# A decoder layer on one core: each layer norm's four normalised tiles shared between GpSimd and ScalarE

## The chip, the cores and the metric

One core of one Trainium2 chip runs the whole kernel in one launch. The time is the device time of that core in microseconds, the median of three runs. In the rows PE is TensorE, PEld its weight load, DVE is VectorE, ACT is ScalarE, POOL is GpSimd and SPq is the queue of SyncE, which issues the DMAs.

## The reference

Four batch entries (b = 0 to 3) of 512 tokens and 128 channels pass through one decoder layer, all in f32. `_layernorm` has no learnt scale or bias.

```python
def _layernorm(x, axis=-1, eps=1e-05):
    m = jnp.mean(x, axis=axis, keepdims=True)
    v = jnp.var(x, axis=axis, keepdims=True)
    return (x - m) / jnp.sqrt(v + eps)

x = x + attn(_layernorm(x))            # causal, 16 heads of 8 channels
x = x + xattn(_layernorm(x), ctx)      # 77 masked context rows, 16 heads
x = x + ffn(_layernorm(x))             # gate, top 2 of 8 experts of 128x128, summed by weight
```

So there are twelve layer norms, named (b, k) here: k = 0 before the causal attention, 1 before the cross attention, 2 before the experts.

## The kernel before

The work is cut into some 530 steps. The string `ORDER` (line 66) holds one letter for each; `chains` (line 73) has a list of steps per letter, and `plan` (line 126) takes the next step of a letter's list each time the letter comes. A step is a triple (kind, b, k). The result, `SCHEDULE`, is one order for the whole program, and **every engine walks it in that order** and does its own part of each step: a loop over `SCHEDULE` stands in the block of SyncE, GpSimd, ScalarE, VectorE and TensorE. Engines meet at semaphores only. Digits in `ORDER` are steps "warm": products of ones on PE (line 929) whose results nobody reads.

PSUM has eight banks. `plan` gives each step on PE that needs one the bank (or pair) that is released earliest in the order, and PE waits in `bank_free` (line 885) until the engine that reads the bank's former contents has counted up `bank_taken`. So an activation or a reduction that reads a bank also decides when PE may begin a later step.

The steps that the text speaks of:

- `ln_stats`: DVE takes the statistics of four tiles of 128 tokens (lines 729 to 736) and signals `var_ready`; POOL makes `rstd` by a power (line 500) and `shift` = −mean · rstd (line 501), four columns each.
- `ln_norm`: POOL makes the four normalised tiles `normed` (line 508), each as state · rstd + shift, and signals `norm_ready`. There are two buffers of `normed`, so from the third norm on it waits for the turn before the last.
- `turn_x`: PE waits for `norm_ready` and transposes the four tiles into a bank (lines 939 to 942, recorded at line 909); ACT copies them to `normed_t` (line 604).
- `peak`: PE makes scores in one layout (lines 1009 and 1014) and DVE reduces them to maxima (line 764); `xpeak` is the same for the cross attention (line 779). Their halves are split by `split_peaks` and `split_xpeaks`.
- `scores`: PE makes the scores transposed, less their maximum, two banks at a time (line 1081); ACT takes the exponential of both banks into `probs` (line 664), 128x1024 each time; POOL masks it (line 558). `xscores` is the same for the cross attention (line 671). `values` and `xvalues` are the products with v (lines 1099 and 1121).
- `turn_mix` (ACT's copy at line 686), `add_attention` (PE at line 901, DVE adds to `state` at line 819), `gate`, `choose` (ACT's exponential at line 689, between two parts of DVE's), `expert` (PE at line 1151, DVE at line 870) and `sum_experts` (POOL at lines 569 and 572).

In the order, `ln_norm` stands 2 to 27 steps behind its `ln_stats` and 1 to 17 steps ahead of its `turn_x`. Before the change ACT has no part in it. Around norm (0, 1) the order is, for instance: ln_stats (0, 1), scores (1, (1, 1)), values, **ln_norm (0, 1)**, scores (1, (1, 2)), two peaks, context_values, scores (1, (1, 3)), values, scores (1, (1, 4)), ln_stats (3, 0), values, scores (1, (2, 0)), scores (1, (2, 1)), a peak, turn_x (0, 1). Norm (2, 1) stands right behind `choose` (0), and norm (3, 1) right behind `choose` (1).

Of the kernel before, what the change touches and what calls it, by code (L numbers as in the profile page):

```python
# [10 lines left out]
ALU = mybir.AluOpType  # L11
ACT = mybir.ActivationFunctionType
# [5 lines left out]
T = S // 128  # L18
# [39 lines left out]

XPROBS = 6
BANKS, CAUSAL_BANKS = 8, (6, 7)  # L60

SUMMED_BY_DVE = ((B - 1, 1), (B - 1, 3))

# [107 lines left out]
def uses(*kinds):  # L171

    return {x: n + 1 for n, x in enumerate(x for x in SCHEDULE if x[0] in kinds)}


STATS = uses("ln_stats")
NORM = uses("ln_norm")
NORMS = list(NORM)


def decoder_layer(nc, x, ctx_t, mask, wq, bq, wk, bk, wq_t, bq_t, wk_t, bk_t, wv, bv, wp, bp, xwq, xwk,
                  xwv, xwo,
                  gate_w, gate_b, expert_w, expert_b, out):
    with ExitStack() as stack:
        def sb(name, shape, dt=F32):
            return stack.enter_context(nc.sbuf_tensor(name, shape, dt))

        def sem(name):
            return stack.enter_context(nc.semaphore(name))
# [36 lines left out]
        state = sb("state", [128, B, T, D])  # L226
# [4 lines left out]
        rstd = sb("rstd", [128, 3 * B, T])  # L231
        lowered = sb("lowered", [128, 3 * B, T])
        shift = sb("shift", [128, 3 * B, T])
        normed = sb("normed", [128, 2, T, D])
# [62 lines left out]
        last_row_ready = sem("last_row_ready")  # L297
        causal_full, causal_ready = sem("causal_full"), sem("causal_ready")
        var_ready, norm_ready = sem("var_ready"), sem("norm_ready")
        bank_full = [sem(f"bank_full{i}") for i in range(BANKS)]  # L300
        bank_taken = [sem(f"bank_taken{i}") for i in range(BANKS)]
        q_ready = sem("q_ready")
# [38 lines left out]
        def bank_of(step, s=0):  # L341
            return banks[:, PLACE[step] + s]
# [4 lines left out]
        def full_of(step):  # L347
            return bank_full[PLACE[step]]

        def taken_of(step):  # L350
            return bank_taken[PLACE[step]]

        def wait_full(eng, step):

            eng.wait_ge(full_of(step), FULL[step])
# [12 lines left out]
        def context_heads_of(b):  # L368
            return xv_s[0:S2, b, VW:].rearrange("p (h c) -> p h c", c=2 * VW)
# [94 lines left out]
        def _(pool):  # L464
            gp = nc.gpsimd
            chain = [0]

            def link(ins):
                chain[0] += 1
                ins.then_inc(pool_chain, 1)  # L470
                pool.wait_ge(pool_chain, chain[0])
# [22 lines left out]
            for step in SCHEDULE:  # L494
                kind, b, k = step
                if kind == "ln_stats":

                    n = 3 * b + k
                    pool.wait_ge(var_ready, STATS[step])
                    link(gp.tensor_tensor(rstd[:, n], var[:, n], minus_half[:], ALU.pow))  # L500
                    link(gp.tensor_tensor(shift[:, n], lowered[:, n], rstd[:, n], ALU.mult))
                elif kind == "ln_norm":
                    n = 3 * b + k
                    i = NORM[step]
                    if i > 2:
                        wait_full(pool, ("turn_x", *NORMS[i - 3][1:]))
                    for t in range(T):
                        last = gp.tensor_scalar(normed[:, i % 2, t], state[:, b, t], rstd[:, n, t:t + 1], shift[:, n, t:t + 1],  # L508
                                                ALU.mult, ALU.add)
                    last.then_inc(norm_ready, 1)  # L510
# [3 lines left out]
                elif kind in PROJECTED:  # L514
                    n = PROJECTED[kind]
# [5 lines left out]
                elif kind in SPLIT:  # L521
                    n = SPLIT[kind]
                    pool.wait_ge(middle_ready[n], b + (2 if n == "x" else 1))
                    gp.tensor_tensor(parts[n][:, 2], rest_of(n, b), parts[n][:, 1], ALU.subtract).then_inc(low_ready[n], 1)
                    if kind == "split_k" and b == 0:
# [5 lines left out]
                        for e in range(E):  # L531
                            last = gp.memset(rank[:, :, e:e + 1], float(E - e))
# [27 lines left out]
                elif kind == "sum_experts" and (b, k) not in SUMMED_BY_DVE:  # L560

                    t = k
# [13 lines left out]
        def _(act):  # L576
            ac = nc.scalar
# [16 lines left out]
            for step in SCHEDULE:  # L594
                kind, b, k = step
                if kind == "context_values":
                    wait_full(act, step)
                    if b == 0:
                        wait_cleared(act, "xv_s")
                    ac.copy(context_heads_of(b)[:, :, 0:DH], bank_of(step)[0:S2, 0:D].rearrange("p (h d) -> p h d", h=H)  # L600
                            ).then_inc(taken_of(step), 1)
                elif kind == "turn_x":
                    wait_full(act, step)
                    ac.copy(normed_t[k][:], bank_of(step)).then_inc(taken_of(step), 1)  # L604
# [4 lines left out]
                elif kind == "project_qt":  # L609
                    act.wait_ge(bias_ready, 1)  # L610
                    wait_full(act, step)
                    for i in range(GROUPS):
                        ac.activation(q_t[:, i], bank_of(step), ACT.Identity, bias=q_bias[:, i:i + 1],
                                      scale=own[:, i:i + 1]).then_inc(q_ready if i < 3 else taken_of(step), 1)
                elif kind in PROJECTED:
                    n = PROJECTED[kind]
# [13 lines left out]
                    else:  # L630
# [5 lines left out]
                        bias = (bq_s if n == "q" else bk_s)[:, 0:1]  # L636
                        ac.activation(parts[n][:, 0], bank_of(step), ACT.Identity, bias=bias).then_inc(high_ready[n], 1)
                        ac.activation(full[n][:], bank_of(step), ACT.Identity, bias=bias).then_inc(taken_of(step), 1)
                elif kind in SPLIT:
                    n = SPLIT[kind]  # L640
# [16 lines left out]
                elif kind == "scores":  # L657
                    grp, u = k
                    wait_full(act, step)
                    n = 4 * b + grp  # L660
# [5 lines left out]
                elif kind == "xscores":  # L666
                    wait_full(act, step)
                    n = H * b + 2 * k
# [213 lines left out]
        def _(pe):  # L882
# [22 lines left out]
            def turn(src, step):  # L905

                bank_free(step)
                for t in range(T):
                    last = te.transpose(bank_of(step)[:, 128 * t:128 * t + 128], src(t), ident[:])  # L909
                last.then_inc(full_of(step), 1)  # L910
# [8 lines left out]
            for c in range(2):  # L919
                last = te.matmul(banks[:, CAUSAL_BANKS[1], 128 * c:128 * c + 128],  # L920
                                 spread_slot[:, c].rearrange("p s r -> p (s r)"), causal[:, 0], start=True, stop=True)
            last.then_inc(causal_full, 1)

            for step in SCHEDULE:
                kind, b, k = step
# [13 lines left out]
                elif kind == "turn_x":  # L939
                    i = NORM[("ln_norm", b, k)]  # L940
                    pe.wait_ge(norm_ready, i)
                    turn(lambda t: normed[:, i % 2, t], step)
                elif kind == "project_kt":
                    wait_taken(pe, ("turn_x", b, 0))
# [21 lines left out]
                elif kind == "tile_peak":  # L966

                    grp, i, j = k
# [20 lines left out]
                    for t, col in TILE_PEAKS[i]:  # L989
                        last = te.matmul(bank[:, col:col + 128 * (t + 1)], lane(q_t, j)[:, grp, 128 * t:128 * t + 128],  # L990
                                         lane(k_t, j)[:, 0:128 * (t + 1)],
                                         start=False, stop=(t, col) == TILE_PEAKS[i][-1], skip_group_check=True)
                    last.then_inc(full_of(step), 1)
                elif kind == "peak":

                    f, u = k
                    t, heads = PEAKS[u]
                    n, width = len(heads), 128 * (t + 1)
# [13 lines left out]
                    for i, p in enumerate(heads):  # L1012
                        for s in range(2):
                            last = te.matmul(bank_of(step, s)[:, width * i:width * i + width],  # L1014
                                             in_slot(q_stack, s, MAX_ROW)[:, b % 2, 4 * f + p, 128 * t:128 * t + 128],
                                             in_slot(k_stack, s, MAX_ROW)[:, b % 2, 4 * f + p, 0:width],
                                             start=False, stop=(i == n - 1), skip_group_check=True)
                            if i == n - 1:
                                last.then_inc(full_of(step), 1)
                elif kind == "xpeak":  # L1020
# [11 lines left out]
                    if b in XDIRECT:  # L1032
# [6 lines left out]
                        for t in range(lo // 4, (hi + 3) // 4):  # L1039
                            first, end = max(lo, 4 * t), min(hi, 4 * t + 4)  # L1040
                            for s in range(2):
                                last = te.matmul(bank_of(step, s)[:, S2 * (first - lo):S2 * (end - lo)],  # L1042
                                                 in_slot(full["x"], s, SLOT)[:, 128 * t:128 * t + 128],
                                                 in_slot(own_keys, s, SLOT)[:, 4 * f + first - 4 * t:4 * f + end - 4 * t],
                                                 start=False, stop=(end == hi), skip_group_check=True)
                                if end == hi:
                                    last.then_inc(full_of(step), 1)
                    else:
                        for i in range(lo, hi):
                            t, p = divmod(i, 4)  # L1050
                            for s in range(2):
                                last = te.matmul(bank_of(step, s)[:, S2 * (i - lo):S2 * (i - lo) + S2],
                                                 in_slot(xq_stack, s, MAX_ROW)[:, b % 2, 4 * f + p, 128 * t:128 * t + 128],
                                                 in_slot(xk_stack, s, MAX_ROW)[:, 4 * f + p, S2 * b:S2 * b + S2],
                                                 start=True, stop=True)
                                if i == hi - 1:
                                    last.then_inc(full_of(step), 1)
                elif kind in ("turn_peaks", "turn_xpeaks"):
# [5 lines left out]
                    for t in range(T):  # L1064
                        last = te.transpose(bank_of(step)[0:16, 64 * t:64 * t + 64].bitcast(BF16),
                                            src[:, k, t].rearrange("p s i a -> p (s i a)"), ident_b[:])
                    last.then_inc(full_of(step), 1)
                elif kind == "scores":
# [9 lines left out]
                    for even, odd in zip(SCORES[2 * u], SCORES[2 * u + 1]):  # L1078
                        for s, (col, j, kt) in enumerate((even, odd)):
                            p, n = (4 * grp + j) // 2, S - 128 * kt  # L1080
                            last = te.matmul(bank_of(step, s)[:, col:col + n],  # L1081
                                             in_slot(k_stack, s)[:, b % 2, p, 128 * kt:128 * kt + 128],
                                             in_slot(q_stack, s)[:, b % 2, p, 128 * kt:S], start=True, stop=True)
                            if even == SCORES[2 * u][-1]:
                                last.then_inc(full_of(step), 1)
                elif kind == "values":
# [9 lines left out]
                    for kt in tiles:  # L1096
                        for j in range(4):
                            slot, col = PROB_PLACE[(kt, j)]
                            last = te.matmul(bank_of(step)[32 * j:32 * j + 2 * VW, 128 * kt:S], padded(v_s[:, b % 2, kt], 4 * grp + j),  # L1099
                                             probs[:, grp % 2, slot, col:col + S - 128 * kt], start=(kt == 0 and grp % 2 == 0),  # L1100
                                             stop=(kt == 2 and grp % 2 == 1), skip_group_check=True)
# [11 lines left out]
                elif kind == "xvalues":  # L1113
# [6 lines left out]
                    for j in range(4):  # L1120
                        last = te.matmul(bank_of(step)[32 * j:32 * j + 2 * VW, :], padded(xv_s[0:S2, b], 4 * k + j),  # L1121
                                         xprobs[0:S2, (H * b + 4 * k + j) % XPROBS], start=(k % 2 == 0), stop=(k % 2 == 1),
                                         skip_group_check=True)
                    last.then_inc(full_of(step), 1)
                elif kind in ("mix", "xmix"):
                    i = int(kind == "xmix")
# [13 lines left out]
                elif kind == "expert_bias":  # L1140
# [4 lines left out]
                    for t in range(T):  # L1145
                        last = te.matmul(bank_of(step)[:, D * t:D * t + D], comb_t[:], expert_b_s[:, t], start=True, stop=True)
                    last.then_inc(full_of(step), 1)
                elif kind == "expert":
                    bank_free(step)
                    t, half = divmod(k, 2)  # L1150
# [47 lines left out]
```

## Time and profile before

| what | value |
|---|---|
| median of three runs | 279.82 us (278.49 to 280.61) |
| the profiled execution | 279.67 us |
| its span in the trace | 277.6 us |
| mean granted clock of TensorE | 0.97 |
| instructions | 6416 |

The span is from the first to the last instruction of the program that the trace holds; the profiled execution's time is 2.07 us longer. Times in rows count from the start of the span.

### The profile page before, as it was taken

How to read it: one execution, taken by the hardware profiler on the slowest of the kernel's cores; microseconds unless marked ns; L12 is line 12 of the kernel's file. 1: busy time of each engine (PE TensorE's matmuls, PEld its weight loads, DVE VectorE, ACT ScalarE, POOL GpSimd, SP SyncE). 2: the span in 40 equal slices, each digit the busy share in tenths (PEclk: the TensorE clock that was granted, in tenths of full speed). 3: DMA queues.
4: the chain of work that ended last, by engine and by line, in shares of the span. 5: the costliest groups of instructions: out<-in, count | busy, mean ns of one | idle time of the engine just before them, and what ended most of it. 6: DMA issues, size and time to landing. Idle time of an engine off the chain costs nothing.

```text
span 277.6 us, 6416 instructions
## 1 busy us (share of the span) xinstructions
PE 253.6 (91%) x2438; PEld 121.3 (44%) x2438; DVE 227.1 (82%) x502; ACT 169.4 (61%) x225; POOL 162.2 (58%) x265
## 2 busy tenths in 40 slices
PE   7799778999998999999999999999999979997990
PEld 3379433434453354454345443345534643343540
DVE  7349999898999999999799998568986797355695
ACT  5183089698887768989979758983566334610000
POOL 5739676845549643766413582375985674059644
PEclk9899999999999999999999999999999995999797
DMA  3743326200440400611300001300003011000101
GB/s 86 208 114 104 104 68 171 61 15 6 109 122 2 113 6 5 183 49 33 85 5 6 2 0 40 81 4 2 5 0 94 21 42 40 2 0 0 38 0 38
DMA packets 19948, 14.32 MB, mean 52 GB/s; under 512 B 2720, under 2 KB 19920, under 8 KB 19920
## 3 DMA queue, kind: packets, MB, share of 16 engines
q1 hardware_dynamic: 19920, 13.94, 18.4%
q8 instruction: 19, 0.31, 0.5%
q14 instruction: 9, 0.07, 0.1%
HBM read 2.58 MB, written 1.05 MB: 13 GB/s over the span
## 4 chain that ended last, share of the span: by engine, by line
PE 46%; DVE 34%; ACT 5%; POOL 5%; issue 4%; SPq 2%; DMA 2%; DVEq 0%; POOLq 0%
DVE peaks L764 10%; PE banks L1099 8%; PE banks L1121 5%; PE banks L897 5%; PE banks L1151 5%; DVE peaks L772 5%; PE banks L1081 4%; PE banks L901 4%; PE banks L909 4%; ACT probs L664 3%; PE banks L1111 2%; DVE xpeaks L779 2%; PE banks L1014 2%; DVE stats L730 2%; DVE yw L870 2%
## 5 line engine op out<-in xcount | busy, mean ns | idle before, releaser
L664 ACT ACTIVATE probs<-banks 128x1024 f32<-128x1024 f32 x80 | 79.8, 1025 | 15.5 <-PE banks L1081 14.4
L764 DVE TENSOR_REDUCE peaks<-banks 128x2 f32<-128x768 f32 (+3 forms) x77 | 82.6, 1119 | 5.0 <-PE banks L1014 4.4
L558 POOL TENSOR_SCALAR_AFFINE_SELECT probs<-probs 128x512 f32<-128x512 f32 (+1 forms) x80 | 43.6, 549 | 52.3 <-ACT probs L664 51.6
L569 POOL TENSOR_TENSOR yw<-yw 128x512 f32<-128x512 f32 (+2 forms) x42 | 34.9, 830 | 22.3 <-DVE yw L870 19.4
L1099 PE MATMUL banks<-probs,v_s 128*18 128x256 f32 (+3 forms) x512 | 42.9, 436 | 0.0
L671 ACT ACTIVATE xprobs<-banks 77x1024 f32<-77x1024 f32 x32 | 31.9, 1017 | 11.7 <-PE banks L1111 11.6
L1151 PE MATMUL banks<-expert_w_s,normed_t 128*128 128x512 f32 x64 | 33.0, 620 | 0.0
L1081 PE MATMUL banks<-q_stack,k_stack 64*128 64x512 bf16 (+3 forms) x256 | 30.1, 300 | 1.8 <-DMA q_stack<-peaks_t 0.6
L779 DVE TENSOR_REDUCE xpeaks<-banks 128x10 f32<-128x770 f32 (+1 forms) x24 | 23.5, 1007 | 5.7 <-PE banks L1042 3.1
L1014 PE MATMUL banks<-k_stack,q_stack 62*128 62x128 bf16 (+3 forms) x224 | 27.3, 297 | 0.0
L870 DVE TENSOR_TENSOR yw<-banks,g_comb 128x512 f32<-128x512 f32 x32 | 20.8, 684 | 5.7 <-PE banks L1151 5.3
L1009 PE MATMUL banks<-causal_slot,pick_slot 64*128 64x64 bf16 (+2 forms) x308 | 19.5, 205 | 2.7 <-DVE peaks L764 1.8
L1009 PEld LDWEIGHTS banks<-causal_slot,pick_slot 64*128 64x128 bf16 x308 | 10.9, 94 | 24.1 <-DVE peaks L764 9.9
L508 POOL TENSOR_SCALAR normed<-state,rstd,shift 128x128 f32<-128x128 f32 x48 | 21.0, 451 | 0.6
L1099 PEld LDWEIGHTS banks<-probs,v_s 128*18 128x18 f32 x512 | 10.9, 97 | 17.6 <-issue 15.1
L1121 PE MATMUL banks<-xprobs,xv_s 77*18 77x512 f32 x128 | 18.3, 645 | 0.1
L1081 PEld LDWEIGHTS banks<-q_stack,k_stack 64*128 64x128 bf16 x256 | 9.4, 94 | 20.5 <-DVE peaks L764 6.7
L500 POOL TENSOR_TENSOR rstd<-var,minus_half 128x4 f32<-128x4 f32 x12 | 12.2, 1015 | 6.7 <-DVE lowered L736 6.7
L604 ACT COPY normed_t<-banks 128x512 f32<-128x512 f32 x12 | 7.0, 586 | 13.9 <-PE banks L909 13.8
L1151 PEld LDWEIGHTS banks<-expert_w_s,normed_t 128*128 128x128 f32 x64 | 10.8, 194 | 9.3 <-issue 8.7
L929 PE MATMUL banks<-ones_b 128*128 128x512 bf16 x46 | 14.1, 438 | 0.5 <-DVE peaks L764 0.5
L772 DVE TENSOR_REDUCE peaks<-banks 128x1 f32<-128x128 f32 (+3 forms) x32 | 12.8, 473 | 0.0
(179 smaller groups left out, 422.3 us busy)
## 6 DMA issues: line engine op xcount, KB each, us to landing
q_stack<-parts_q SPq DMA_DIRECT2D x24, 128.0 KB, 2.4
k_stack<-parts_k SPq DMA_DIRECT2D x24, 128.0 KB, 2.4
xq_stack<-parts_x SPq DMA_DIRECT2D x24, 128.0 KB, 2.4
state<-in_x SPq DMA_DIRECT2D x4, 256.0 KB, 4.9
out<-state SPq DMA_DIRECT2D x4, 256.0 KB, 2.3
expert_w_s<-in_expert_w SPq DMA_DIRECT2D x1, 512.0 KB, 4.3
xk_stack<-parts_x SPq DMA_DIRECT2D x6, 77.0 KB
q_stack<-peaks_t SPq DMA_DIRECT2D x16, 8.0 KB
```

Source lines behind the costliest of these rows:

```text
L558: gp.affine_select(out=v, in_=v, compare_op=ALU.is_ge, fill=0.0, base=0, pattern=pattern, channel_multiplier=-1).then_inc(causal_done, 1)
L569: link(gp.tensor_tensor(y[:, 0:n], y[:, 0:n], y[:, n:2 * n], ALU.add))
L664: ac.activation(probs[:, grp % 2, 2 * u:2 * u + 2, :], both_banks(step), ACT.Exp, scale=SCALE).then_inc(taken_of(step), 1)
L671: ac.activation(xprobs[0:S2, n % XPROBS:n % XPROBS + 2, :], both_banks(step)[0:S2], ACT.Exp, scale=SCALE).then_inc(taken_of(step), 1)
L764: ve.tensor_reduce(peaks[:, f, t, heads[0]:heads[0] + n].rearrange("p a s -> p s a"), both_banks(step)[:, :, 0:n * width].rearrange("p s ( ...
L779: ve.tensor_reduce(xpeaks[:, f].rearrange("p s t a -> p s (t a)")[:, :, lo:hi], both_banks(step)[:, :, 0:(hi - lo) * S2].rearrange("p s (h ...
L1009: te.matmul(half, in_slot(pick_slot, s, SLOT)[:, 128 * c:128 * c + 128], in_slot(causal_slot, s, SLOT)[:, c].unsqueeze(1).broadcast_to([SL ...
L1014: last = te.matmul(bank_of(step, s)[:, width * i:width * i + width], in_slot(q_stack, s, MAX_ROW)[:, b % 2, 4 * f + p, 128 * t:128 * t + 128],
L1081: last = te.matmul(bank_of(step, s)[:, col:col + n], in_slot(k_stack, s)[:, b % 2, p, 128 * kt:128 * kt + 128], in_slot(q_stack, s)[:, b % ...
L1099: last = te.matmul(bank_of(step)[32 * j:32 * j + 2 * VW, 128 * kt:S], padded(v_s[:, b % 2, kt], 4 * grp + j), probs[:, grp % 2, slot, col: ...
L1121: last = te.matmul(bank_of(step)[32 * j:32 * j + 2 * VW, :], padded(xv_s[0:S2, b], 4 * k + j), xprobs[0:S2, (H * b + 4 * k + j) % XPROBS], ...
L1151: te.matmul(bank_of(step), normed_t[2][:, 128 * t:128 * t + 128], expert_w_s[:, 4 * half:4 * half + 4].rearrange("d e f -> d (e f)"), star ...
```

## The change

Four things change. POOL's `shift` instruction now signals a semaphore `shift_ready`, in place of a link in POOL's own chain. In `ln_norm` POOL waits for it and makes tiles 0 and 1 only. ACT gets a part of `ln_norm`, at that step's place in the order: it waits for the buffer (from the third norm on) and for `shift_ready`, makes tiles 2 and 3 as `Identity` activations with the scale `rstd` and the bias `shift`, and signals `norm_ready_by_act`. PE's `turn_x` waits for both signals. `ORDER` stays as it is.

```diff
+NORM_BY_POOL, NORM_BY_ACT = (0, 1), (2, 3)
...
+        shift_ready, norm_ready_by_act = sem("shift_ready"), sem("norm_ready_by_act")
...
                     link(gp.tensor_tensor(rstd[:, n], var[:, n], minus_half[:], ALU.pow))
-                    link(gp.tensor_tensor(shift[:, n], lowered[:, n], rstd[:, n], ALU.mult))
+                    gp.tensor_tensor(shift[:, n], lowered[:, n], rstd[:, n], ALU.mult).then_inc(shift_ready, 1)
                 elif kind == "ln_norm":
                     n = 3 * b + k
                     i = NORM[step]
                     if i > 2:
                         wait_full(pool, ("turn_x", *NORMS[i - 3][1:]))
-                    for t in range(T):
+                    pool.wait_ge(shift_ready, STATS[("ln_stats", b, k)])
+                    for t in NORM_BY_POOL:
                         last = gp.tensor_scalar(normed[:, i % 2, t], state[:, b, t], rstd[:, n, t:t + 1], shift[:, n, t:t + 1],
                                                 ALU.mult, ALU.add)
                     last.then_inc(norm_ready, 1)
...
+                elif kind == "ln_norm":
+                    n = 3 * b + k
+                    i = NORM[step]
+                    if i > 2:
+                        wait_full(act, ("turn_x", *NORMS[i - 3][1:]))
+                    act.wait_ge(shift_ready, STATS[("ln_stats", b, k)])
+                    for t in NORM_BY_ACT:
+                        last = ac.activation(normed[:, i % 2, t], state[:, b, t], ACT.Identity, bias=shift[:, n, t:t + 1],
+                                             scale=rstd[:, n, t:t + 1])
+                    last.then_inc(norm_ready_by_act, 1)
                 elif kind == "turn_x":
...
                     pe.wait_ge(norm_ready, i)
+                    pe.wait_ge(norm_ready_by_act, i)
                     turn(lambda t: normed[:, i % 2, t], step)
```

## Rows read from the trace of the kernel before

**Rows 1.** Busy time in stretches: us, then PE, PEld, DVE, ACT, POOL, PEclk, DMA

```profile
0.00:277.60 277.60, 253.65 (x2438) 121.30 (x2438) 227.12 (x502) 169.41 (x225) 162.17 (x265) 0.97 0.19 52
...
81.00:88.00 7.00, 6.54 (x92) 2.76 (x84) 6.83 (x24) 6.34 (x8) 5.09 (x10) 1.00 0.01 2
```

**Rows 2.** The chain that ended last, share of the span by engine

```profile
PE 46%; DVE 34%; ACT 5%; POOL 5%; issue 4%; SPq 2%; DMA 2%; DVEq 0%; POOLq 0%
```

**Rows 3.** Timeline around norms (0, 0) and (3, 2): start, us, engine, what, [idle before]

```profile
9.78 0.44 PE L909 MATMUL banks<-ident,normed 128*128 128x128 f32 x2 [1.28 <-POOL normed L508]
...
253.52 1.74 POOL L508 TENSOR_SCALAR normed<-state,rstd,shift 128x128 f32<-128x128 f32 x4
...
255.31 0.66 PE L909 MATMUL banks<-ident,normed 128*128 128x128 f32 x4 [1.74 <-POOL normed L508]
```

**Rows 4.** ACT's groups by form: xcount | busy us, mean ns | idle before

```profile
L604 ACT COPY normed_t<-banks 128x512 f32<-128x512 f32 x12 | 7.0, 586 | 13.9 <-PE banks L909 13.8
...
L613 ACT ACTIVATE yw<-banks,q_bias,own 128x512 f32<-128x512 f32 x4 | 2.8, 776 | 1.0 <-PE banks L897 1.0
...
L600 ACT COPY xv_s<-banks 77x128 f32<-77x128 f32 x4 | 1.1, 271 | 0.5 <-PE banks L937 0.4
```

**Rows 5.** Timeline of ACT behind norm (3, 0) and behind norm (2, 2)

```profile
97.82 1.02 ACT L664 ACTIVATE probs<-banks 128x1024 f32<-128x1024 f32 x1 [0.94 <-PE banks L1081]
...
226.29 1.02 ACT L671 ACTIVATE xprobs<-banks 77x1024 f32<-77x1024 f32 x1 [4.36 <-PE banks L1111]
```

**Rows 6.** Timeline of ACT and POOL around norm (2, 0)

```profile
51.05 1.02 ACT L664 ACTIVATE probs<-banks 128x1024 f32<-128x1024 f32 x1 [0.69 <-PE banks L1081]
...
50.92 0.20 POOL L501 TENSOR_TENSOR shift<-lowered,rstd 128x4 f32<-128x4 f32 x1
```

**Rows 7.** Timeline of ACT, POOL, PE and DVE around norm (0, 1)

```profile
81.96 1.02 ACT L664 ACTIVATE probs<-banks 128x1024 f32<-128x1024 f32 x1
...
83.85 0.20 POOL L501 TENSOR_TENSOR shift<-lowered,rstd 128x4 f32<-128x4 f32 x1
...
83.04 0.39 PE L1081 MATMUL banks<-q_stack,k_stack 64*128 64x128 bf16 x4
...
87.38 1.21 DVE L764 TENSOR_REDUCE peaks<-banks 128x4 f32<-128x1024 f32 x1
```

**Rows 8.** Timeline of ACT, POOL and DVE around norm (1, 1)

```profile
121.17 1.03 ACT L664 ACTIVATE probs<-banks 128x1024 f32<-128x1024 f32 x1
...
122.73 0.20 POOL L501 TENSOR_TENSOR shift<-lowered,rstd 128x4 f32<-128x4 f32 x1
...
123.55 1.21 DVE L764 TENSOR_REDUCE peaks<-banks 128x4 f32<-128x1024 f32 x1
```

**Rows 9.** Timeline of ACT and PE around norms (0, 2) and (2, 1)

```profile
160.15 1.02 ACT L671 ACTIVATE xprobs<-banks 77x1024 f32<-77x1024 f32 x1 [0.23 <-PE banks L1111]
...
166.67 0.23 ACT L689 ACTIVATE g_exp<-g_shifted 128x32 f32<-128x32 f32 x1 [2.06 <-DVE g_shifted L834]
...
166.31 0.66 PE L909 MATMUL banks<-ident,normed 128*128 128x128 f32 x4
```

**Rows 10.** Timeline of ACT, POOL and DVE around norm (1, 2)

```profile
194.45 1.02 ACT L671 ACTIVATE xprobs<-banks 77x1024 f32<-77x1024 f32 x1 [1.41 <-PE banks L1111]
195.91 0.58 ACT L686 COPY mixed_t<-banks 128x512 f32<-128x512 f32 x1 [0.44 <-PE banks L909]
...
195.69 0.20 POOL L501 TENSOR_TENSOR shift<-lowered,rstd 128x4 f32<-128x4 f32 x1
...
198.33 0.69 DVE L819 TENSOR_TENSOR state<-banks,state 128x512 f32<-128x512 f32 x1
```

**Rows 11.** Busy time in stretches, columns as in rows 1

```profile
226.60:229.90 3.30, 2.17 (x18) 1.59 (x18) 1.90 (x4) 2.70 (x4) 2.90 (x5) 1.00 0.00 0
230.00:236.70 6.70, 6.70 (x27) 1.28 (x26) 5.58 (x24) 2.27 (x3) 2.69 (x4) 0.50 0.13 42
```

**Rows 12.** What PE's turns of the normed tiles waited for: us, times

```profile
  POOL normed L508: 12.9, 11
```

## The prediction

> **What bounds the kernel now.** I read the busy time of the whole span first [rows 1]: the reader is to see that no engine is idle for long, PE above all (253.65 of 277.60 us), then DVE (227.12), while ACT and POOL have 108 and 115 us to spare. Then the chain that ended last [rows 2]: almost half of it is PE, a third DVE, ACT and POOL 5% each. So average load says that ACT could take 24 small operations for nothing. But the stretch from 81 to 88 us, in which a layer norm falls, shows ACT busy for 6.34 of 7.00 us beside DVE at 6.83 [rows 1]: what counts there is the order in each queue, so I read the timelines around each of the 12 norms last. I write (b, k) for the norm k of batch entry b.
>
> The profiled execution took 279.67 us for a span of 277.6; the median of the three runs is 279.82, so I add my sum to 279.67 and take the two as the same.
>
> **What an operation costs.** POOL makes its four tiles in 1.74 us [rows 3] at the last norm, about 0.44 each; two are left, so POOL is done 0.88 us sooner, 12 times. The activation of a 128x128 tile with a scale and a bias from memory isn't in the trace. Nearest rows [rows 4]: a plain copy of 128 columns takes 0.271 us, one of 512 columns 0.586, the activation of 512 columns with both vectors 0.776. The vectors thus cost 0.19, and I take 0.46 for one. Four of the long ones keep ACT 2.8 us busy, 0.1 less each than their durations, so I take 0.82 for the pair; the bounds are 0.5 (two plain copies, overlapping) and 1.5 (two of the long ones). 24 of these add some 10 us to ACT's 169.41.
>
> The Trainium skill, Perfetto Trace Analysis, section Optimizing GPSIMD Operations, says to prefer other engines, since GpSimd is generally slower. The trace doesn't bear this out for this operation: 0.44 us on POOL against 0.46 estimated on ACT. By the rule the move would be a gain for its own sake; by the rows it is one only where both halves run at once.
>
> **Where the halves do run at once.** Norm (0, 0): PE stood idle for 1.28 us until POOL's last tile, and its turn starts at 9.78 [rows 3]; ACT had nothing to do. Both halves are there 0.88 us sooner: −0.9 us, and the chain goes on through PE and DVE, so it stays. Norm (3, 2), at the end: PE idle for 1.74 us for it [rows 3], ACT idle: −0.9 us again, up to the last store. Norm (1, 0) finds ACT idle, and what follows waits for DVE: 0. Norm (3, 0): ACT reaches it at 96.87 (97.82 less the idle 0.94), the shift is long ready, and 0.82 fits before the activation that had to wait for PE anyhow [rows 5]: 0. Norm (2, 2): ACT had 4.36 us idle before 226.29 [rows 5], and PE would be freed by 0.3, but what is next, the split maxima of the cross attention, waits for DVE: 0.
>
> **Where ACT comes too early.** The other seven have the step ahead of the activations that PE and DVE live on, and ACT is in order: behind its new wait stand the exponentials that empty the PSUM banks, behind those PE (in order too) for a bank, and DVE for PE's next maxima.
>
> Norm (2, 0): ACT is free at 50.36 (51.05 less the idle 0.69), the shift ends at 51.12, so the next scores start at about 52.0 instead of 51.05 [rows 6]. Their bank is wanted by PE a step later; DVE has maxima in hand. I take +0.4 (0 to 1).
>
> Norm (0, 1): ACT goes straight from one exponential to the next at 81.96, but the shift ends at 84.05 [rows 7]. The tiles are done at 84.95 and scores(1, (1, 2)) runs to 86.0 instead of 82.98, 3.0 us later. PE's scores step at 83.04 takes that very bank, so PE stands until 86.1. Then ACT has three more exponentials of 1.02 us one behind the other (they end at 87.6, 88.9, 89.8); PE's next peak step needs the bank of the second, starts at 88.95, and DVE's reduction of it, at 87.38, becomes 89.5: +2.1, because DVE had 1 us of statistics in hand. From there PE's next steps wait for DVE's reductions, so 2.1 is what goes on.
>
> Norm (1, 1): ACT goes on without idle time at 121.17, the shift ends at 122.93 [rows 8], tiles done at 123.85; scores(2, (1, 4)) starts 2.7 us later and frees its bank at 124.9. PE's next peak step takes that bank, and DVE's reduction of it, at 123.55, moves to 125.5: +2.0. The two exponentials behind are late by 2.3 to 2.7. I take +2.1.
>
> Norms (0, 2) and (2, 1): ACT reaches the first at 159.92, 0.82 of tiles where 0.23 was idle, so the activations behind it are 0.6 late, PE with them (it has no idle time to give back here). The second stands behind the gate's exponential, which ends at 166.90 because DVE gave its input late; PE's turn of those tiles was at 166.31 [rows 9]. It becomes 167.2 + 0.9 + 0.1 = 168.2: +1.9 for both, on PE, which is back to back from there to 190 us.
>
> Norms (1, 2) and (3, 1): ACT is free at 193.04 (194.45 less the idle 1.41), the shift ends at 195.89, tiles 196.8, and then the exponential that had run from 194.45 ends at 197.8. The copy of the mixed heads at 195.91 starts there: +1.9, PE's projection waits for it (+2.0), and the residual's addition on DVE, which begins at 198.33 [rows 10] on a bank that was ready some 0.6 us before, moves by +1.4. Stats, gate and top-2 follow, +1.6 where DVE releases the first expert bank. Norm (3, 1) is behind the gate's exponential as (2, 1) was, 1 us more on ACT, but PE is held by DVE later. I take +1.6.
>
> Sum: −0.9 − 0.9 + 0.4 + 2.1 + 2.1 + 1.9 + 1.6 = +6.3 us.
>
> **The clock.** PE gets new idle times of 3.0, 2.2 and 2.0 us in full speed stretches. In the kernel before, PE was busy for 2.17 of the 3.30 us up to 229.9, and the stretch after it, 230 to 236.7 us, was granted 0.50, that is 1.2 GHz in place of 2.4 [rows 11]. The Trainium skill, TensorE: Matmul & The Clock Gate, section Part 1: The HAM clock gate, has the gate follow how busy PE has recently been; the trace agrees, by this row. A stall of 3 us is a bigger hole than that one. What a fall costs: PE works 6.7 us at half speed, so between 0 (where DVE or ACT sets the pace) and 3.3 us each. I take 1.4 us in all, one fall that is half felt. Total +7.7: 287.4 us.
>
> POOL's 10 us are worth nothing but this: its masks and expert sums come 0.9 us sooner behind a norm, and the values steps that wait for masks then wait for ACT.
>
> **Rivals.** (a) *Absorbed waits.* The stalls are real but PE and DVE take back half of them between norms. For it: ACT idles about 108 us in all. Against it: PE and DVE, which would have to catch up, are at 6.54 and 6.83 of 7.00 around a norm [rows 1]. Half of 8.1 less 1.8 is +2.3 to +3.5: 282 to 283.2 us. (b) *Falls of the clock at each of the three long stalls,* fully felt, 1.7 to 3 us each: 6.3 + 6: 292 us. (c) *Faster: parallel halves decide.* PE was idle for 12.9 us before 11 turns, waiting for POOL's last tile [rows 12]; if ACT's halves are always there first, four turns on the chain and the two ends give 0.88 each, and the delayed exponentials cost less than that: 279.7 − 4 × 0.88 = 276.2 us. It decides only if ACT reaches its step no earlier than about 1 us before the shift; the rows show 2.1, 1.8 and 2.85 us at three norms, and at two it is behind the gate's exponential instead. (d) *Nothing:* the two ends (−1.8) pay for what isn't absorbed: 279 to 281 us. (e) The pair costs 1.5 us: that is in the range.
>
> **Chances.** The forecast (284.5 to 290.5) 0.58; (a) 0.20; (b) 0.09; (c) 0.05; (d) 0.08. The range, 282.4 to 292.3, takes in (a)'s upper half and most of (b), and the bounds of the pair. A per cent is 2.8 us, about what a measurement of this kernel can tell from no change: above 282.6 us lie the forecast, (b) and most of (a), 0.85; below 277.0 lies (c), 0.05; 0.10 between.
>
> **What would show it.** Per step: POOL's groups with 24 tiles of 0.44 us; ACT's new group of 24 at 0.4 to 0.5 us, with idle time before it of about 0.8 + 2.2 + 1.7 + 2.9 us at the four and more at idle places, released by POOL's shift; PE before scores (L1081's successor) waiting for ACT's probs at about 83 to 86 us; the start 0.9 us sooner up to 50 us; PE's clock at 0.5 in a stretch soon after a stall. DVE busy time unchanged, its idle time up by some 7 us. The prediction is wrong if DVE's reduction after norm (0, 1) is under 1 us late against the start's gain, if ACT's wait at (0, 1) or (1, 1) is under 1 us, or if the ends gain nothing.

## The result, and the profile after

The changed kernel took 285.2 us in the median of four runs (284.64 to 286.82), the kernel before 279.15 (276.67 to 280.61) beside it: a ratio of 1.0253, with a 95% interval of 1.0199 to 1.0308 (the quotient of the two medians is 1.0217). It is slower, by 2.5% where 2.8% was forecast (7.7 on 279.67), and the time lies in the range. Here and below, executions more than 1.5% above the fastest of their kernel stay in the medians and are left out of the ratios. The profiled execution took 285.58 us.

Busy time over the span, the lines of the page that say where load went (columns: busy us, share, instructions; then tenths of full clock in 40 slices), with the chain that ended last and three groups:

```profile
span 283.6 us, 6422 instructions
PE 252.2 (89%) x2433; PEld 120.6 (43%) x2438; DVE 227.3 (80%) x502; ACT 179.1 (63%) x249; POOL 152.1 (54%) x241
PEclk9999999999986999997999999999999999899998
PE 44%; DVE 30%; ACT 10%; POOL 7%; issue 6%; SPq 1%; DMA 1%; ACTq 0%; POOLq 0%; DVEq 0%
L779 DVE TENSOR_REDUCE peaks<-banks 128x2 f32<-128x768 f32 (+3 forms) x77 | 82.6, 1120 | 14.1 <-PE banks L1030 13.5
L1097 PE MATMUL banks<-q_stack,k_stack 64*128 64x512 bf16 (+3 forms) x256 | 31.3, 310 | 4.5 <-ACT probs L679 2.9
L614 ACT ACTIVATE normed<-state,shift,rstd 128x128 f32<-128x128 f32 x24 | 10.5, 486 | 25.9 <-POOL shift L505 25.8
```

Against [rows 1] and [rows 2]: 10 us of work went from POOL (162.17 to 152.11) to ACT (169.41 to 179.15), as meant; PE and DVE do what they did. But ACT's share of the chain doubled, and DVE's peak reductions, the group with the most busy time, now stand idle for 14.1 us, 13.5 of them until PE's scores; in the kernel before it was 5.0. The last row is ACT's new group: 0.486 us for one activation, and 25.8 us of idle time that POOL's shift ended, at eight norms. 17.9 of these fall on (0, 0), (1, 0), (2, 2) and (3, 2), where ACT had nothing else to do; 0.85, 2.30, 1.75 and 2.96 us fall on (2, 0), (0, 1), (1, 1) and (1, 2). PEclk shows two dips in the middle, at slices 12 to 13 and 19, that the kernel before had not.

The timeline of the changed kernel around norm (0, 1), ACT, POOL, PE and DVE (start, us, engine, what, [idle before <-releaser]), answers to [rows 7]:

```profile
78.73 1.01 ACT L679 ACTIVATE probs<-banks 128x1024 f32<-128x1024 f32 x1
82.03 0.88 ACT L614 ACTIVATE normed<-state,shift,rstd 128x128 f32<-128x128 f32 x2 [2.30 <-POOL shift L505]
82.82 1.00 ACT L679 ACTIVATE probs<-banks 128x1024 f32<-128x1024 f32 x1
...
81.74 0.20 POOL L505 TENSOR_TENSOR shift<-lowered,rstd 128x4 f32<-128x4 f32 x1
...
83.87 0.61 PE L1097 MATMUL banks<-q_stack,k_stack 64*128 64x128 bf16 x4 [2.94 <-ACT probs L679]
84.41 1.91 PE L1115 MATMUL banks<-probs,v_s 128*18 128x384 f32 x16
...
89.53 2.95 DVE L779 TENSOR_REDUCE peaks<-banks 128x4 f32<-128x1024 f32 x3 [4.91 <-PE banks L1030]
```

The reader is to see the whole mechanism in the brackets: ACT idle for 2.30 us until POOL's shift, PE idle for 2.94 until ACT's exponential frees a bank, DVE idle for 4.91 until PE has made its scores. PE's first matmuls behind the stall take 0.61 us where the same ones took 0.39 [rows 7]: the clock has fallen.

Busy time in stretches around the two stalls (columns as in rows 1):

```profile
80.00:82.90 2.90, 0.94 (x20) 0.50 (x12) 2.87 (x9) 0.86 (x3) 2.17 (x5) 1.00 0.02 6
83.00:89.70 6.70, 5.83 (x46) 1.89 (x47) 1.72 (x11) 4.26 (x6) 3.08 (x5) 0.50 0.00 0
...
122.00:127.20 5.20, 3.17 (x40) 1.88 (x34) 3.48 (x13) 3.45 (x6) 3.47 (x7) 1.00 0.01 3
127.30:130.60 3.30, 3.30 (x28) 0.89 (x24) 1.69 (x4) 2.51 (x3) 0.79 (x2) 0.50 0.00 0
```

Behind each of the two stalls, in which PE was busy for a third and for three fifths of the time, a stretch was granted 0.50 (1.2 GHz in place of 2.4), 6.7 and 3.3 us long. In the first DVE fell to 1.72 of 6.70 us, while PE, once it had the bank at 83.87, was busy to the end: PE is the bound there.

### The profile page after: what moved, and what is told of

It reads as the page before. It is cut to its first block, busy times and chain, and to the rows that moved or that the text cites. A ratio compares the mean times of both kernels' runs of the same rounds, so it can differ in the third digit from the quotient of the medians.

```text
span 283.6 us, 6422 instructions
## 1 busy us (share of the span) xinstructions
PE 252.2 (89%) x2433; PEld 120.6 (43%) x2438; DVE 227.3 (80%) x502; ACT 179.1 (63%) x249; POOL 152.1 (54%) x241
## 4 chain that ended last, share of the span: by engine, by line
PE 44%; DVE 30%; ACT 10%; POOL 7%; issue 6%; SPq 1%; DMA 1%; ACTq 0%; POOLq 0%; DVEq 0%
PE banks L1115 9%; DVE peaks L779 8%; PE banks L912 5%; PE banks L1137 5%; PE banks L1097 5%; DVE peaks L787 4%; ACT probs L679 4%; PE banks L916 4%; PE banks L924 3%; PE banks L1167 3%; PE banks L1030 3%; POOL yw L574 3%; PE banks L1025 2%; POOL rstd L504 2%; DVE xpeaks L794 2%
## 5 line engine op out<-in xcount | busy, mean ns | idle before, releaser
L779 DVE TENSOR_REDUCE peaks<-banks 128x2 f32<-128x768 f32 (+3 forms) x77 | 82.6, 1120 | 14.1 <-PE banks L1030 13.5
L1115 PE MATMUL banks<-probs,v_s 128*18 128x256 f32 (+3 forms) x512 | 45.1, 456 | 0.0
L1097 PE MATMUL banks<-q_stack,k_stack 64*128 64x512 bf16 (+3 forms) x256 | 31.3, 310 | 4.5 <-ACT probs L679 2.9
L614 ACT ACTIVATE normed<-state,shift,rstd 128x128 f32<-128x128 f32 x24 | 10.5, 486 | 25.9 <-POOL shift L505 25.8
L1137 PE MATMUL banks<-xprobs,xv_s 77*18 77x512 f32 x128 | 17.2, 609 | 0.1
L1167 PEld LDWEIGHTS banks<-expert_w_s,normed_t 128*128 128x128 f32 x64 | 10.5, 189 | 9.1 <-issue 8.4
L1127 PE MATMUL banks<-xq_stack,xk_stack 64*77 64x512 bf16 x64 | 12.5, 406 | 0.0
L1006 PE MATMUL banks<-mix_t,yw 32*128 32x256 f32 (+3 forms) x64 | 12.2, 442 | 0.0
```

The source lines that it names most:

```text
L779: ve.tensor_reduce(peaks[:, f, t, heads[0]:heads[0] + n].rearrange("p a s -> p s a"), both_banks(step)[:, :, 0:n * width].rearrange("p s ( ...
L1097: last = te.matmul(bank_of(step, s)[:, col:col + n], in_slot(k_stack, s)[:, b % 2, p, 128 * kt:128 * kt + 128], in_slot(q_stack, s)[:, b % ...
L1167: te.matmul(bank_of(step), normed_t[2][:, 128 * t:128 * t + 128], expert_w_s[:, 4 * half:4 * half + 4].rearrange("d e f -> d (e f)"), star ...
```

## The experiments

Three theories. **A**: ScalarE comes to its new step before the shift is there, waits in order, and TensorE stalls behind it for a bank; the loss is those waits and the slow stretches that follow (a slow stretch: one in which TensorE's granted clock is 0.50). **B**: the 10.5 us of new work on ScalarE cost. **C**: the stalls alone cost, the clock has no part. The edits are shown against the changed kernel.

**e1: the wait without the work.** ACT's wait for the buffer and its signal are gone too.

```diff
-                    for t in NORM_BY_POOL:
+                    for t in range(T):
...
                     act.wait_ge(shift_ready, STATS[("ln_stats", b, k)])
-                    for t in NORM_BY_ACT:
...
-                    pe.wait_ge(norm_ready_by_act, i)
```

> GpSimd makes all four tiles again, as before the change; ScalarE only waits for the shift at its ln_norm step and makes nothing. Theory A (ScalarE's wait at the step's place in the order costs, and TensorE's stalls behind it cost more by a lower clock): the exponential after norm (0, 1) starts some 2.1 us late and DVE's next peak reduction 1.2 us or more, the same at (1, 1); without the gains at start and end (2.3 and 0.7 us in the changed kernel's trace) the time is 283 to 287 us, at least +1.3% on the kernel before. Theory B (the 10.5 us of new work on ScalarE cost): no work is added, so 279 to 280.5 us.

**e2: the work without the wait.** ACT's activations read and write buffers of their own, which no one else reads.

```diff
-                    for t in NORM_BY_POOL:
+                    for t in range(T):
...
                 elif kind == "ln_norm":
...
-                    act.wait_ge(shift_ready, STATS[("ln_stats", b, k)])
                     for t in NORM_BY_ACT:
-                        last = ac.activation(normed[:, i % 2, t], state[:, b, t], ACT.Identity, bias=shift[:, n, t:t + 1],
-                                             scale=rstd[:, n, t:t + 1])
+                        ac.activation(unread[:, t - 2], lent[:, 0], ACT.Identity, bias=lent[:, 1, 0:1], scale=lent[:, 1, 1:2])
...
-                    pe.wait_ge(norm_ready_by_act, i)
```

> GpSimd makes all four tiles; ScalarE makes two activations of 128x128 with scale and bias from memory at each ln_norm step, from a buffer of its own into one that nobody reads, with no wait. Theory A: 0.87 us at each place, most of it inside the 1 us that DVE has in hand or inside ScalarE's idle time: 279.5 to 281.5 us, under +0.8%. Theory B: about the changed kernel's +2% or more, 284 to 286 us.

Measured: e1 281.95 us, 1.0106 (1.0043 to 1.0170); e2 278.56 us, 1.0046 (1.0011 to 1.0082). The same 24 activations, 10.5 us busy at 0.486 each in e2 as in the changed kernel, cost half a per cent; B falls, and e2 is 0.9 us under the times that A gave, its ratio within A's +0.8%. e1's +1.1% is under the +1.3% that I had put as A's least, and its time under the 283 us: the waits alone cost less than forecast. Its trace says why. At (0, 1) of e1, ACT and DVE:

```profile
82.69 1.02 ACT L673 ACTIVATE probs<-banks 128x1024 f32<-128x1024 f32 x1 [2.24 <-POOL shift L505]
...
87.19 1.22 DVE L773 TENSOR_REDUCE peaks<-banks 128x4 f32<-128x1024 f32 x1 [1.77 <-PE banks L1023]
```

ACT waits 2.24 us, against 2.30 in the changed kernel, but without the tiles' 0.88 behind it DVE idles for 1.77 us, and no slow stretch follows at (0, 1) or (1, 1). So wait and work together make what neither does alone.

**e3: only norm (0, 1) shared**, the other eleven by POOL alone (`SHARED = ((0, 1),)` in the conditions of all three engines).

> Only norm (0, 1) is shared, the other eleven are GpSimd's alone. Theory A with the clock: ScalarE's wait of 2.2 us and its tiles put DVE 2.1 us back, and a stretch at granted clock 0.5 right behind the stall adds about 2 more: 283 to 284.5 us. Theory C (stalls alone, the clock without part): +2.1, 281.5 us, with no slow stretch at 83 to 90 us. Theory B: +0.1, no change.

**e4: the stall filled.** The changed kernel, with 13 products of ones on PE ahead of `context_values` 3, the last thing that PE does before the stall. They write that step's bank, which the step then overwrites. The trace holds 12 of the 13.

```diff
                 elif kind == "context_values":
                     bank_free(step)
+                    for _ in range(13 * (b == B - 1)):
+                        te.matmul(bank_of(step), ones_b[:, 0:128], ones_b[:], start=True, stop=True)
```

> The changed kernel with 13 products of ones on TensorE ahead of context_values 3, so inside the stall behind norm (0, 1); their bank is that step's own and nobody reads them. If the slow stretch that begins at 82.9 us is due to the stall, it goes and the changed kernel gains about 2 us: 283 us, with DVE after norm (0, 1) about 2.2 instead of 4.3 us later against the stretch ahead of it. Theory C: the same time as the changed kernel, 285 us or more.

Measured: e3 282.25 us, 1.012 (1.0049 to 1.0191); e4 282.36 us, 1.0125 (1.0060 to 1.0191), so 2.8 us under the changed kernel's median though it does more; the intervals of the two ratios do not meet. The mean granted clock was 0.986 to 0.992 in the four executions of e4, 0.965 to 0.977 in the four of the changed kernel. The stretches of e4 (first two lines) and of e3 (columns as above):

```profile
80.00:83.00 3.00, 2.84 (x32) 1.59 (x30) 2.93 (x9) 0.70 (x3) 1.98 (x4) 1.00 0.05 11
83.00:89.70 6.70, 6.06 (x71) 2.67 (x70) 3.95 (x14) 6.04 (x9) 4.27 (x9) 1.00 0.01 2
```

```profile
81.00:84.20 3.20, 0.26 (x2) 0.03 (x3) 3.17 (x10) 1.84 (x4) 2.42 (x5) 1.00 0.01 3
84.30:87.60 3.30, 3.30 (x32) 0.82 (x31) 0.61 (x3) 1.36 (x2) 1.19 (x2) 0.50 0.00 0
```

With PE kept busy through the stall (2.84 of 3.00 us) the clock stays at 1.00, and ACT works for 6.04 of the next 6.70 us where it managed 4.26. ACT waits 2.30 us as before; DVE after it idles for 2.68 us instead of 4.91:

```profile
81.01 2.75 PE L953 MATMUL banks<-ones_b 128*128 128x512 bf16 x12 [0.16 <-issue]
...
87.59 2.09 DVE L779 TENSOR_REDUCE peaks<-banks 128x4 f32<-128x1024 f32 x2 [2.68 <-PE banks L1032]
```

The Trainium skill, TensorE: Matmul & The Clock Gate, section Part 1: The HAM clock gate, says that the gate's ratio is set by how busy PE has been recently; e3, with PE busy for 0.26 of 3.20 us ahead of the fall, and e4 beside the changed kernel bear that out. It is not the whole account: e1's stall at (0, 1), with PE busy for 1.65 of the 3.50 us from 80 to 83.5, had no fall behind it. C falls. e3's median is below what A expected (283 us); the kernel before took 277.9 us beside it, which makes +4.4 by the medians and +3.3 by the ratio. In the trace the norm costs 3.7.

**e8: only norm (1, 1) shared.**

> Only norm (1, 1) is shared. Theory A with the clock: DVE about 2.1 us late behind it, and 0 to 1.5 us more by a slow stretch if one follows: 280 to 281.5 us against 278 before. Theory C (stalls without the clock): +2.1, 280 us.

Measured: 282.58 us, 1.0161 (1.0112 to 1.0210), +4.6, above both expectations: a slow stretch followed here too, at 127.3 us as in the changed kernel, and another at 89.7 us, where no norm is shared. The stretch ahead of it, then DVE and POOL in it, in e8:

```profile
86.30:89.70 3.40, 1.92 (x23) 1.03 (x22) 3.40 (x4) 2.84 (x4) 3.15 (x7) 1.00 0.00 0
```

```profile
86.12 1.78 DVE L752 TENSOR_SCALAR var<-moments 128x4 f32<-128x4 f32 x1
...
86.06 1.82 POOL L565 TENSOR_SCALAR_AFFINE_SELECT probs<-probs 128x512 f32<-128x512 f32 x3
```

DVE's small operation took 1.78 us, to the end of POOL's masks, where it took 0.73 in the first trace of before, and PE then waited 1.07 us for DVE's peaks (0.54 there). PE was busy for 1.92 us of the 3.40 ahead of the fall; in the first trace of before it was 2.45 at the same place, and no fall followed. Why DVE's operation was long was not tried.

**e7: ACT's part moved to where the shift is ready.** The part is a function, called behind ACT's own part of a step given by its place in `SCHEDULE`; all twelve norms are shared, and `ORDER` and the other engines are as in the changed kernel. Six norms get a new place; the other six keep theirs.

```diff
+ACT_BEHIND = {(0, 1): 155, (1, 1): 244, (2, 0): 80, (1, 2): 409, (2, 1): 341, (3, 1): 422}
...
+            places = {ACT_BEHIND.get(x[1:], SCHEDULE.index(x)): x[1:] for x in NORMS}
+            for place, step in enumerate(SCHEDULE):
...
+                if place in places:
+                    norm_by_act(*places[place])
```

> All norms shared as in the changed kernel, but ScalarE's part of six norms stands later or earlier in its order, where the shift is ready: (2,0) behind scores(0,(1,4)), (0,1) behind scores(1,(1,3)), (1,1) behind xscores(0,1), (2,1) ahead of the gate's exponential, (1,2) behind turn_mix(3), (3,1) behind xscores(2,3). Theory A: the places, not the sharing, made the loss; ScalarE's waits fall under 0.3 us each, the stalls and the slow stretches at 83 and 127 us go, 276 to 279 us, no slower than the kernel before by more than 0.5%. Theory B (the work or the second semaphore costs): 283 us or more.

**e9: only the norms that find ACT idle.** `SHARED = ((0, 0), (1, 0), (3, 0), (2, 2), (3, 2))`.

> Only the five norms at which ScalarE stands idle are shared: (0,0), (1,0), (3,0), (2,2), (3,2). Theory A: 0.9 us gained at the start and 0.7 at the end and nothing lost: 276 to 277.5 us against about 278 before, -0.3 to -0.8%. Theory B: +0.3 or more.

**e10: ACT's part as late as can be**, as e7, with the place right ahead of `turn_x` for every norm.

> All norms shared, ScalarE's part at each norm right ahead of its own copy of the turned tiles, the latest place that can be. No wait for the shift is left then; in its stead TensorE waits in its order for ScalarE to come there, 1 to 2 us at each norm where ScalarE runs behind TensorE. Theory A: better than the changed kernel, worse than the placed one: 279 to 284 us.

Measured: e7 274.74 us, 0.9892 (0.9853 to 0.9931); e9 276.11 us, 0.9937 (0.9906 to 0.9969); e10 298.72 us, 1.0705 (1.0641 to 1.0770). e7 beats the changed kernel by 10.5 us (3.7%) with the same work on every engine, and the kernel before by 1.1%: better than the 276 to 279 us that I expected of it. e9 came as expected; its interval and e7's overlap, so it isn't shown that sharing the other seven norms is worth anything. e10 is far above its 279 to 284. ACT, then POOL, around norm (0, 1) in e7:

```profile
81.40 1.02 ACT L682 ACTIVATE probs<-banks 128x1024 f32<-128x1024 f32 x1 [0.15 <-PE banks L1102]
82.32 0.87 ACT L607 ACTIVATE normed<-state,shift,rstd 128x128 f32<-128x128 f32 x2
83.09 2.83 ACT L682 ACTIVATE probs<-banks 128x1024 f32<-128x1024 f32 x3
...
81.75 0.20 POOL L506 TENSOR_TENSOR shift<-lowered,rstd 128x4 f32<-128x4 f32 x1
```

The shift is there at 81.95 and ACT at 82.32: nobody waits. ACT has no idle time before its tiles at any of the six moved norms. And e10, ACT and PE at the same norm:

```profile
90.02 2.85 ACT L682 ACTIVATE probs<-banks 128x1024 f32<-128x1024 f32 x3 [0.29 <-PE banks L1102]
92.75 0.88 ACT L607 ACTIVATE normed<-state,shift,rstd 128x128 f32<-128x128 f32 x2
...
93.73 0.72 PE L929 MATMUL banks<-ident,normed 128*128 128x128 f32 x4 [2.12 <-issue]
```

Now ACT's three exponentials stand ahead of its tiles, and PE, which runs ahead of ACT, stands idle for 2.12 us before the turn (the profile names no releaser there; the tiles end at 93.63). The stall has only changed its cause, and it now comes at nearly every norm: before ten turns of the normed tiles PE's matmuls waited 17.8 us in all, 0.45 to 2.12 at nine of them, about as expected, and 4.35 at (1, 0), where ACT's copy behind DVE's context keys is late. The mean granted clock was 0.948 in that execution, 0.970 in the first trace of before.

**e11: the kernel before once more**, and **e12: e7 with norm (0, 2) by POOL alone.**

> The kernel before once more, unchanged, for a second trace. If the slow stretch at 11.5 us belongs to the kernel it is there again, with TensorE's later work at the same times; if it only falls that way in some executions, as the gain of 1.4 us at the start of four experiments suggests, it may be gone, the span 1 to 2 us shorter and everything between 20 and 225 us earlier by 1.4 us in one piece.

> As e7_moved, but norm (0, 2), the one that was not moved and still put DVE and TensorE 0.44 us back, is made by GpSimd alone. Theory A: that 0.44 us is gained, 274.3 us, -1.3% against the kernel before; if the time is not lower than e7_moved's 274.7 by more than its interval tells, the step's offset in the trace decides.

Measured: e11 277.01 us (one run), a span of 275.0 where the first trace had 277.6. e12 274.51 us, 0.9891 (0.9837 to 0.9945): in time not to be told from e7. In the trace it stays at −0.58 through norm (0, 2), where e7 rises from −0.63 to −0.20, so the 0.4 us are gained there as expected (table below). The first trace of before (first line) and e11 (second), around the start:

```profile
11.60:14.80 3.20, 3.20 (x5) 1.33 (x4) 0.00 (x0) 0.85 (x2) 0.48 (x2) 0.50 0.60 151
```

```profile
10.20:13.40 3.20, 2.74 (x10) 1.16 (x8) 0.00 (x0) 1.48 (x3) 1.88 (x2) 1.00 0.89 252
```

One kernel, and its first slow stretch is there in one execution and absent in the other. So e11, which has no slow stretch before 229 us, is the better base for traces. **Where each kernel stands against e11**, in us: the start of the same instruction in both traces, subtracted (a rise from one row to the next is lost between them; the instructions are DVE's, in the row of norm (0, 2) one of ACT's):

| after | e11 itself | first trace | changed | e1 wait | e2 work | e3 (0,1) | e4 filled | e8 (1,1) | e7 moved | e12 |
|---|---|---|---|---|---|---|---|---|---|---|
| norm (0, 0) | 31.22 | +1.44 | −0.86 | +0.07 | 0.00 | +0.01 | −0.41 | +1.71 | −0.23 | −0.56 |
| norm (2, 0) | 77.85 | +1.82 | −0.28 | +0.43 | −0.10 | +0.03 | 0.00 | +1.79 | −0.28 | −0.23 |
| norm (0, 1) | 102.11 | +1.83 | +3.99 | +1.84 | −0.23 | +3.75 | +2.23 | +3.88 | −0.63 | −0.58 |
| norm (1, 1) | 140.47 | +1.83 | +7.48 | +3.31 | +0.20 | +3.69 | +6.04 | +7.38 | −0.63 | −0.57 |
| norm (0, 2) | 158.33 | +1.83 | +7.92 | +3.35 | +0.64 | +3.69 | +6.47 | +7.37 | −0.19 | −0.58 |
| norm (2, 1) | 175.90 | +1.83 | +9.06 | +3.35 | +0.62 | +3.69 | +7.61 | +7.38 | −0.20 | −0.58 |
| norm (3, 1) | 206.19 | +1.82 | +10.40 | +4.01 | +0.85 | +3.82 | +8.88 | +7.53 | −0.28 | −0.68 |
| last expert | 269.25 | +2.56 | +8.61 | +4.92 | +1.70 | +4.69 | +5.72 | +7.11 | −2.12 | −2.56 |

The reader is to see steps, and flat stretches between them: a loss of 2.23 at 92 us in e4 is still 2.23 at 120. Up to 225 us hardly anything is taken back. (The rises of e4 and e8 at norm (1, 1), 3.81 and 3.50, have a slow stretch in them as the changed kernel's has; e1's, 1.47, has none. e8's rise of 2.1 at norm (0, 1), which it doesn't share, is DVE's late operation and the slow stretch at 89.7.)

## Why the prediction was right, point by point

- *What an operation costs.* POOL's two tiles 0.88 us as forecast, ACT's pair 0.88 against 0.82: the short copy's 0.271 and the 0.19 between the long activation and the long copy gave 0.46 for one, and 0.486 was measured.
- *Where the halves run at once.* The start gained 0.86 us (forecast 0.9), and 0.88 in e9; in the traces of e4, e7 and e12, which share norm (0, 0) as well, it gained 0.41, 0.23 and 0.56. There PE's 15 products of ones ahead of the turn took longer, 4.34 us in e7 where the changed kernel's took 3.40, and the turn began at 9.60 instead of 8.93 us. So this gain is not there in every execution. At the end PE's idle time before norm (3, 2) went from 1.74 [rows 3] to 0.98, a gain of 0.76 of the 0.9. Norms (1, 0) and (3, 0) moved nothing, as forecast. Norm (2, 2), forecast at nothing, gained DVE's gate 0.75 us (10.40 to 9.65), of which 0.2 was left at 237 us.
- *Norm (2, 0):* +0.6 (−0.86 to −0.28), forecast +0.4. But in the changed kernel most of it is not the forecast path. PE waited 0.57 us for a DMA, before ACT's tiles even began at 48.96, and 0.17 for ACT later. The same DMA cost 0.44 us in the first trace of before and 0.41 in e1. In e4, where PE did not wait for it, the forecast wait came, 0.64 us, and 0.4 was lost (−0.41 to 0.00). So +0.4 is borne out by e4 alone. PE in the changed kernel, then in e4:

```profile
48.04 0.40 PE L1025 MATMUL banks<-causal_slot,pick_slot 64*128 64x256 bf16 x4 [0.57 <-DMA k_stack<-parts_k]
```

```profile
51.21 0.23 PE L1027 MATMUL banks<-causal_slot,pick_slot 64*128 64x64 bf16 x4 [0.64 <-ACT probs L679]
```

- *Norm (0, 1):* the stall alone, as e4 shows it with the clock held up, +2.23, forecast +2.1, by the path forecast: ACT 2.30 us of wait, PE at the bank of the late exponential, DVE with its statistics in hand and then idle.
- *Norm (1, 1):* DVE's reduction there started 4.15 us later than [rows 8] where all before it had been 2.16 later, so the stall made +2.0, forecast +2.1. Its wait is 1.75 us, forecast 1.7.
- *Norms (0, 2) and (2, 1):* +1.6 (7.48 to 9.06), forecast +1.9; in e7, where the tiles of (2, 1) go ahead of the gate's exponential, the second norm costs nothing.
- *Norms (1, 2) and (3, 1):* +1.3, forecast +1.6, with a wait of 2.96 us, forecast 2.9.
- *The clock* is the term that was mis-sized. I took 1.4 us, "one fall that is half felt". Two fell: at (0, 1) the changed kernel lost 4.27 us, 2.0 more than e4, and at (1, 1) 3.49, 1.5 more than its stall, 3.5 in all. The 2.0 is shown by e4; the 1.5 is an estimate, since no run held the clock up at (1, 1), and e1, without a fall there, also lost 0.4 us behind that reduction: it may be 1.1. Part came back: from 225 us to the last expert the changed kernel had one slow stretch where e11 had two, and from 10.40 to 8.61 it gained 1.8 us, of which norm (3, 2) explains 0.76 and norm (2, 2) 0.2.
- *The sum.* Against e11 the changed kernel is 8.6 us longer in the trace, against the first trace of before 6.1, since that one had a slow stretch at its start and a longer one at 230 us. My 7.7 lies between, as does the 7.1 that the ratio gives on 279.67; the medians differ by 6.05. That the total comes this near is partly luck: the clock took more than I gave it and the profiled execution of before was itself a long one.

Rival (a), half of the stalls absorbed, is refuted by the flat stretches; (b), falls fully felt at three stalls, was partly so: two fell. (c), that the halves side by side decide, had the sign right for e7, which meets the condition that I named (ACT no earlier than about 1 us before the shift). But its price rests on a misreading: the 12.9 us at 11 turns [rows 12] add the waits of the weight loads to those of the matmuls. For PE's matmuls alone the trace of before has

```profile
  POOL normed L508: 4.8, 4
```

and these four are (0, 0), (1, 0), (2, 2) and (3, 2), 1.28, 1.49, 0.31 and 1.74 us. At the other eight norms PE's matmuls never waited for POOL's last tile, so sharing could gain little there. The table agrees: from 31 to 206 us e7 gains 0.05 us on e11, and nearly all of its gain comes behind that, where its slow stretch at 253 us is also half as long as e11's.

## What to carry to other kernels

Work moved to an engine with 39% idle time can cost more than it saves, if it is put ahead of what others wait for: price a new wait by when the engine comes to that place in its order, not by its load. Too early and the waiting engine blocks what stands behind it; too late and the reader of the result blocks; a few steps between made +2.5% into −1.1%. And where a stall empties TensorE for some us, look at the granted clock behind it before adding up: at norm (0, 1) the fall cost 2.0 us on top of a stall of 2.2. Last, ask first what there is to gain: TensorE's matmuls waited for the normed tiles at four norms of twelve, and sharing the five at which ScalarE stood idle (e9) gave −0.6% without a new place for anything.

## What the runs showed of the hardware that was not expected

The same kernel before, run twice with a profile, differs by 2.6 us of span: 1.44 is one slow stretch at 11.6 us that only one of them had, 0.38 comes at norm (2, 0), where PE waited 0.44 us for a DMA in the first trace alone, and 1.6 comes with the slow stretch at 230 us, 6.8 us long in the first trace and 3.4 in e11, less 0.8 that is taken back behind it; its 11 to 17 runs beside the experiments lie between 276.3 and 280.8 us. Apart from such stretches the traces repeat closely: e2 and e11 differ by 0.00 at 31 us, and the first trace of before keeps its 1.81 to 1.83 against e11 from 50 to 225 us. Slow stretches without a stall of 2 us ahead of them came too: e8's at 89.7 us, and one each in e3 and e9 at 203.7 and 199.8 us, where PE had been busy for 3.07 of the 3.40 us ahead and no norm near is shared. What brings these on was not tried, so how busy PE was does not by itself tell here whether a fall follows.
